# A two-layer pairwise block: the input projections of both layers rewritten as two row tiles

## The reference, cut to what matters

```python
x = x + conv(_ln_c(x), L0...)          # layer 0
t = t + scan(_ln_t(t))                 # recurrent, over 1024 steps
x = x + conv(_ln_c(x), L1...)          # layer 1
t = t + experts(_ln_t(t))

def conv(z, mask, ...):
    m  = mask[..., None]
    zn = _layer_norm(z, ln_in_w, ln_in_b)
    a  = m * sigmoid(zn @ w_ag + b_ag) * (zn @ w_ap + b_ap)
    b  = m * sigmoid(zn @ w_bg + b_bg) * (zn @ w_bp + b_bp)
    p  = einsum('bikc,bjkc->bijc', a, b)
    x  = _layer_norm(p, ln_out_w, ln_out_b) @ w_z + b_z
    g  = sigmoid(zn @ w_g + b_g)
    return x * g
```

## Time and profile before

| | us |
|---|---|
| median of 3 runs | 2461.65 (2459.01 to 2465.18) |
| profiled execution, whole / span | 2468.82 / 2467.1 |
| project, layer 0: first to last product | 44.7 to 365.8 |
| project, layer 1: first to last product | 1112.3 to 1509.2 |
| share of the span: PE, PEld, DVE, ACT, POOL | 80%, 53%, 67%, 41%, 56% |

### The profile page before, as it was taken

One profiled execution on the slowest core, in us unless ns is written; L12 is line 12 of the kernel. 1 busy time (PEld: TensorE's weight loads), 2 busy tenths in 40 slices (PEclk: granted clock), 3 DMA queues, 4 the chain that ended last, 5 costly groups with the idle time before them and its releaser, 6 DMA issues. The chain is left out here.

```text
span 2467.1 us, 47350 instructions
## 1 busy us (share of the span) xinstructions
PE 1973.2 (80%) x11760; PEld 1303.4 (53%) x11760; DVE 1640.9 (67%) x4305; ACT 1015.5 (41%) x2240; POOL 1380.7 (56%) x1657
## 2 busy tenths in 40 slices
PE   4999994888846668928989884888774899999998
PEld 2555553777732227815555552788763444444443
DVE  3777760555667778827777763166573788888887
ACT  1555551333314557903444432333323555444541
POOL 3999980566766760007777773177685434333330
PEclk9999996999988998959999997999976789998999
DMA  1565644888853321945777673698865555555552
GB/s 50 140 162 144 168 130 128 254 282 276 276 180 99 96 77 41 192 105 176 205 207 207 190 230 99 176 311 296 277 223 159 154 150 157 150 154 155 157 141 74
DMA packets 479516, 422.52 MB, mean 171 GB/s; under 512 B 229036, under 2 KB 376492, under 8 KB 479404
## 3 DMA queue, kind: packets, MB, share of 16 engines
q1 hardware_dynamic: 354476, 253.42, 37.8%
q10 hardware_dynamic: 124928, 167.81, 20.2%
HBM read 236.56 MB, written 150.99 MB: 157 GB/s over the span
## 5 line engine op out<-in xcount | busy, mean ns | idle before, releaser
L532 PE MATMUL cp_pv<-cp_weight,cp_zt 128*128 128x512 f32 x1024 | 536.0, 606 | 0.8 <-ACT cp_zt L563 0.8
L256 POOL TENSOR_TENSOR cc_ln_rstd<-cc_ln_var,numbers 128x8 f32<-128x8 f32 x128 | 255.5, 1996 | 196.8 <-DVE cc_ln_var L247 187.6
L256 POOL TENSOR_TENSOR cp_ln_rstd<-cp_ln_var,numbers 128x8 f32<-128x8 f32 x128 | 228.6, 1786 | 239.9 <-DVE cp_ln_var L247 238.6
L1467 DVE TENSOR_TENSOR ex_xe<-ex_spread,ex_xd 128x512 f32<-128x512 f32 x512 | 322.9, 683 | 40.5 <-PE ex_spread L1709 39.8
L719 PE MATMUL cc_sum<-a_res,cc_bch 128*128 (+1 forms) x2048 | 300.9, 296 | 58.4 <-DMA cc_bch<-b_scratch 56.3
L581 ACT ACTIVATE cp_sig<-cp_pv 128x256 f32<-128x256 f32 x512 | 193.7, 383 | 369.8 <-PE cp_pv L532 354.3
L533 PEld LDWEIGHTS cp_pg<-cp_weight,cp_zt 128*128 128x128 f32 x1024 | 198.3, 194 | 252.0 <-issue 252.0
L424 DVE TENSOR_TENSOR cp_prod<-cp_pv,cp_sig 128x256 f32<-128x256 f32 x512 | 207.2, 419 | 161.6 <-ACT cp_sig L581 133.9
L719 PEld LDWEIGHTS cc_sum<-a_res,cc_bch 128*128 128x128 f32 x2048 | 270.6, 205 | 82.4 <-issue 74.5
L809 ACT ACTIVATE cc_p<-cc_sum 128x512 f32 (+1 forms) x128 | 135.9, 1061 | 382.2 <-PE cc_sum L719 262.6
L1726 PE MATMUL ex_po<-ex_xe,ex_expert 128*64 128x512 f32 x1024 | 272.4, 656 | 0.1
(11 more groups left out here) (209 smaller groups left out, 3274.2 us busy)
## 6 DMA issues: line engine op xcount, KB each, us to landing
cc_bch<-b_scratch SPq DMA_DIRECT2D x256, 256.0 KB, 3.9
gate_scratch<-cp_gs ACTq DMA_DIRECT2D x128, 256.0 KB, 2.5
b_scratch<-cp_b_stage SPq DMA_DIRECT2D x256, 128.0 KB, 2.8
cc_g<-gate_scratch ACTq DMA_DIRECT2D x128, 256.0 KB, 4.5
after_conv<-cc_p ACTq DMA_DIRECT2D x128, 256.0 KB, 3.8
ex_xd<-ex_xt SPq DMA_DIRECT2D x256, 128.0 KB, 2.5
cp_x<-in_x SPq DMA_DIRECT2D x64, 256.0 KB, 3.3
cc_p<-in_x ACTq DMA_DIRECT2D x64, 256.0 KB, 3.6
```

Source lines behind the costliest of these rows:

```text
L256: pool.tensor_tensor(rstd[q][:], var[q][:], numbers[:, 0:1].to_broadcast([P, tiles]), ALU.pow).then_inc(scaled if shifts else known, 1)
L532: pe.matmul(pv[i][:], tokens, weight[:, 0:8 * C], start=True, stop=True).then_inc(v_made, 1)
L1467: dve.tensor_tensor(xe[u.mod(2)][:, :, h, i * P:(i + 1) * P], pb[2 * (p % 2) + h][:].rearrange("p (e t) -> p e t", e=EP), xd[u.mod(8)][:, ...
```

## The change

The project stage is rewritten; the rest is kept but for the layout of b in DRAM.

- **Weights.** The host packs the five matrices, gain, offset and biases of each layer into one array; `fold_weights` loads it with one DMA and folds it with one matmul. The weight is now the same 64 x 320 matrix on partitions 0 to 63 and 64 to 127.
- **Projections.** A row is two matmuls of 64 contraction rows and 320 columns, one for each half h, into two PSUM banks. Three such pairs of banks (`pv`) are taken in turn; `tp` and `ty` have a bank each.
- **One sigmoid.** ACT makes `ag`, `bg` and `g` of a row in one instruction of 384 numbers into `sig`, of which there are two (one per unit in turn). The gate is stored straight from `sig`, and on SP's queue; the sum of layer 1 is stored on SP's queue too.
- **Products and masks.** DVE writes the products of a row straight into `a_res` and `b_stage` (two instructions of 128 numbers), and POOL multiplies both by the mask in place (512 numbers once, 256 numbers twice for each unit).
- **The norm.** Statistics of four units are gathered. DVE makes a first guess of the reciprocal square root from the bits (three instructions of 32 numbers), POOL refines it by three Newton steps and makes a lift (14 instructions of 32 numbers for four units). ACT normalises the rows of half 0 and DVE those of half 1, four instructions of 64 numbers each per unit.
- **Order.** All engines run the same step s (`unit_steps`, loop body of 16 steps), each with its own offsets; x has eight buffers, y one.
- **b in DRAM** is laid out `[chunk, p, k, block, i, c]`; it is stored in four pieces of 256 KB per half and block, and a chunk is read in pieces of 1 KB.

```diff
-                    pe.matmul(pv[i][:], tokens, weight[:, 0:8 * C], start=True, stop=True).then_inc(v_made, 1)
-                    ins = pe.matmul(pg[q][:, i * 2 * C:(i + 1) * 2 * C], tokens, weight[:, 8 * C:],
-                                    start=True, stop=True)
...
+                    for h in range(H):
+                        half = slice(h * HALF, (h + 1) * HALF)
+                        pe.matmul(pv[slot(u, i)][:, h, 0:COLS], zt[u.mod(2)][half, i * P:(i + 1) * P], weight[half, :],
+                                  start=True, stop=True).then_inc(v_made, 1)
...
+                def gates(u, i):
...
+                    if i == 0 and (u - 2).real:
+                        act.wait_ge(gate_stored[u.mod(2)], u.div(2) * 16)
+                        act.wait_ge(prod_made, (u.n - 1) * R)
+                    act.wait_ge(v_made, (u.n * R + i + 1) * H)
+                    act.activation(sig[u.mod(2)][:, :, :, i, :].rearrange("p k h c -> p h k c"),
+                                   pv[slot(u, i)][:, :, 0:3 * C].rearrange("p h (k c) -> p h k c", k=3),
+                                   ACT.Sigmoid).then_inc(sig_made, 1)
...
+                def store_sum(u):
...
+                    sp.wait_ge(summed, u.n + 1)
+                    sp.dma_start(x[:, :, row_block(u), :], xs[u.mod(8)][:]).then_inc(sum_stored[u.mod(8)], 16)
+
+                def store_gate(u):
...
+                    sp.wait_ge(sig_made, u.n * R + R)
+                    sp.dma_start(gate_dram[:, :, row_block(u), :], sig[u.mod(2)][:, 2]).then_inc(gate_stored[u.mod(2)], 16)
...
+                def step(s):
+                    load(s + 9)
+                    store_sum(s + 8)
+                    store_gate(s - 1)
+                    store_b(s - 1)
```

The four other engines run these steps (VectorE, GpSimd, ScalarE, TensorE):

```diff
+                def step(s):
+                    product(s, 0)
+                    normalise(s + 2)
+                    product(s, 1)
+                    add_y(s + 8)
+                    measure(s + 8)
+                    product(s, 2)
+                    product(s, 3)
+                    if s.mod(4) == 3:
+                        first_guess(s + 5)
...
+                def step(s):
+                    mask_a(s - 1)
+                    if s.mod(4) == 0:
+                        refine(s + 4, 0)
+                    if s.mod(4) == 1:
+                        refine(s + 3, 1)
+                    mask_b(s - 1)
...
+                def step(s):
+                    gates(s, 0)
+                    gates(s, 1)
+                    normalise(s + 2, 0)
+                    gates(s, 2)
+                    take(s + 1)
+                    gates(s, 3)
+                    normalise(s + 2, 1)
...
+                def step(s):
+                    project(s, 0)
+                    turn_y(s + 8)
+                    project(s, 1)
+                    flip(s + 1)
+                    project(s, 2)
+                    project(s, 3)
```

More of the change, by code:

```diff
@@ L272, in quads, with __init__, __add__, __sub__ @@
         unit(G - 4 + j, G // 4 - 1, j, 3 - j)
-def quads_peeled(eng, unit):
-    for j in range(4):
-        unit(j, 0, j, 3, j > 0)
-    with eng.Fori(1, G // 4 - 1) as t:
-        for j in range(4):
-            unit(t * 4 + j, t, j, 3, True)
-    for j in range(4):
-        unit(G - 4 + j, G // 4 - 1, j, 3 - j, True)
-def conv_project(nc, tag, x, mask, w, a_res, b_dram, gate_dram, ident, numbers, parts=None):
-    W_COLS = 10 * C
+class Unit:
+    def __init__(self, turn, base, looped, body):
+        self.turn, self.base, self.looped, self.body = turn, base, looped, body
+    def __add__(self, k):
+        return Unit(self.turn, self.base + k, self.looped, self.body)
+    def __sub__(self, k):
+        return self + -k
+    def div(self, m, k=0):
+        return self.turn * (self.body // m) + (self.base + k) // m
+    def mod(self, m):
+        return self.base % m
+    @property
+    def n(self):
+        return self.turn * self.body + self.base
+    @property
+    def real(self):
+        return self.looped or 0 <= self.base < G
@@ new lines, in unit_steps, with fold_weights, _ @@
+def unit_steps(eng, step, first, last, head, tail, body=8):
+    for s in range(first, first + head):
+        step(Unit(0, s, False, body))
+    turns = (last + 1 - tail - first - head) // body
+    with eng.Fori(0, turns) as t:
+        for j in range(body):
+            step(Unit(t, first + head + j, True, body))
+    for s in range(first + head + body * turns, last + 1):
+        step(Unit(0, s, False, body))
+def fold_weights(nc, tag, packed, cols, weight, bank):
+    with Scope(nc, tag) as m:
+        pack = m.sb("pack", [P, P + 2 + cols])
+        fold = m.sb("fold", [P, P])
+        loaded, made, folded = m.sem("loaded"), m.sem("made"), m.sem("folded")
+        with nc.Block() as block:
+            @block.sync
+            def _(sp):
+                sp.dma_start(pack[:], packed).then_inc(loaded, 16)
+            @block.vector
+            def _(dve):
+                dve.wait_ge(loaded, 16)
+                dve.tensor_scalar(fold[:], pack[:, 0:P], pack[:, P:P + 1], pack[:, P + 1:P + 2], ALU.mult, ALU.add
+                                  ).then_inc(made, 1)
+                dve.wait_ge(folded, 1)
+                dve.tensor_scalar(weight, bank[:, 0:cols], 1.0 / C, None, ALU.mult).then_inc(made, 1)
+            @block.tensor
+            def _(pe):
+                pe.wait_ge(made, 1)
+                pe.matmul(bank[:, 0:cols], fold[:], pack[:, P + 2:], start=True, stop=True).then_inc(folded, 1)
@@ new lines, in step @@
+                def step(s):
[3 more added lines that the diff above has]
+                    store_b(s - 1)
+                run(sp, step)
+                for q in range(2):
+                    sp.wait_ge(b_stored[q], B_STORED * (NB // 2))
+                    sp.wait_ge(gate_stored[q], 16 * (G // 2))
+                if parts:
+                    for q in range(8):
+                        sp.wait_ge(sum_stored[q], 16 * (G // 8))
@@ L462, in _, with add_y @@
-                quads(dve, unit)
+                def add_y(u):
+                    if not parts or not u.real:
+                        return
+                    dve.wait_ge(x_in[u.mod(8)], u.div(8) * 16 + 16)
+                    dve.wait_ge(y_turned, u.n + 1)
+                    to = xs[u.mod(8)][:].rearrange("p h i c -> p i h c")
+                    dve.tensor_tensor(to, ty[:].rearrange("p (i h c) -> p i h c", i=R, h=H), to, ALU.add
+                                      ).then_inc(summed, 1)
@@ L538, in _ @@
-                if parts:
-                    pe.sem_inc(zt_made, 1)
-                turn_y(0, 0, 0)
-                turn_y(1, 0, 1)
-                flip(0, 0)
-                turn_y(2, 0, 2)
-                def unit(u, t, j, ahead):
-                    if ahead > 2:
-                        turn_y(u + 3, t + (j + 3) // 4, (j + 3) % 4)
-                    for i in range(R):
-                        if i == 2 and ahead:
-                            flip(u + 1, (j + 1) % 2)
-                        project(u, j % 2, i)
```

511 lines of the change are left out of this document (259 added, 252 removed).

## The result

The changed kernel takes 2471.3 us (median of 20 runs, 2457.52 to 2479.49), the kernel before 2462.9 (20 runs, 2453.37 to 2472.74): a ratio of 1.0034, 95% interval 1.0020 to 1.0047. It is slower by 8 us, where 29 were forecast. The sign was right and the size was not, and the stages show that the small number is a sum of large ones. The table takes the stages out of the two profiled executions, which lie 1 us apart and not 8 (2468.82 and 2469.76 us); "forecast" is the term of the prediction.

A forecast was written before the change was run, and what follows sets the result against it. VectorE was to pace layer 0 and a ring through the gate's store layer 1. Terms 12 + 38 - 17 - 8 - 4 + 8 = +29 us gave 2498 on the profiled execution, 2491 on the median; range 2390 to 2550.

The forecast's parts named there:

- What bounds the kernel, and what is relieved: Project stage: TensorE and GpSimd are full before; afterwards a row on two tiles takes 0.58 us and TensorE is no bound.
- Starts and ends: Before the first product: -17 us in layer 0, -8 in layer 1; ends of both layers' products: -4 together.
- Layer 0, the turns: Layer 0 products: VectorE and GpSimd wait out each other's instructions, normalising takes 2.1 us, a unit 5.2; +12 us.
- I take no change: TensorE's granted clock in the project stage: it stays as it was, as a stretch busy 64% ran at 1.00.
- The ring of 6.8: Layer 1 products: sigmoids wait for the gate's store, queued behind the sum's store and VectorE's add; 6.8 us a unit, +38.
- The combine stages: Both combine stages read b in 1 KB pieces: between 0 and 17 us more, the middle taken, +8.
- No turns: Rival: normalising is let through between GpSimd's instructions, layer 0 products 294 us, whole 2433 or 2439; chance 0.20.
- The ring doesn't bind: Rival, layer 1: stores land sooner, VectorE bounds it at 5.9 us a unit, 378 us, whole 2434; chance 0.14.
- The case of both: Rival: normalising is let through and layer 1 is not held by the gate's store; some 2390 us; chance 0.06.
- Strided writes: Rival: VectorE pays for strided products into `a_res`, 0.44 us a unit in layer 0 (+28), +14 in layer 1; 2533; chance 0.08.
- The gate's store lands late: Rival, layer 1: the store takes 3.5 us in place of 2.6, a unit 7.7, 58 us more; 2549; chance 0.05.
- Tiles that don't overlap: Rival: TensorE needs 5.0 and 5.6 us a unit, hidden, 2491 still; chance 0.05, together with a faster case.

The follow-up runs named there:

- e4: Changed kernel with VectorE's four normalising instructions moved from behind the unit's first product to behind its third; 2399.4 us, ratio 0.9723.
- e6: Changed kernel without GpSimd's masks (a's multiplication left out, b's cut to four numbers a unit), order and waits kept; 2429.8 us, ratio 0.9855.
- e2: Kernel before the change with only the new layout of b, so chunks are read in pieces of 1 KB; 2495.2 us, ratio 1.0105.

## Why the prediction was wrong in size

**What bounds the kernel, and what is relieved.** Right. TensorE and GpSimd were full and are not; the row on two tiles has a pitch of 0.54 us against 0.58 from the earlier trace rows.

**Starts and ends.** Right to a microsecond: -17.7 for -17, -7.3 for -8, -3.5 for -4 (the earlier trace rows against a first product at 27.0 in layer 0 and 39.0 us into layer 1).

**Layer 0, the turns.** The mechanism was right (e4, e6), the size was not. Up to the last look-ahead a unit takes 4.96 us for 5.2: the normalising is 1.63 us on average in place of 2.1, since the mask of a takes 1.04 and not 1.3, and the products of a row have a pitch of 0.41 for 0.45. VectorE was forecast to be full, and is busy 87% of the time. Part of the unit is a cost that the prediction ruled out: one unit in four takes 6.4 us on average, and behind ten of TensorE's fourteen pauses the clock is at half, 44 us in all. "I take no change" of the clock rested on the mean busy share of one stretch, 64% at full clock; here the share is higher (76%) and the clock still falls. With the late normalising it is 77%, one pause is over 1.5 us, and the clock stays at 1.00. The mean share was no ground for the forecast.

**The step that failed in both layers: a steady period times 64.** The last seven or eight units have nothing to load, add or measure, and nothing to normalise for later. Two of them in layer 0, one unit apart:

```profile
325.08 0.38 DVE L528 TENSOR_TENSOR a_res<-cp_pv,cp_sig 128x128 f32<-128x128 f32 x1 [0.84 <-ACT cp_sig L657]
...
329.10 0.39 DVE L528 TENSOR_TENSOR a_res<-cp_pv,cp_sig 128x128 f32<-128x128 f32 x1 [0.84 <-ACT cp_sig L657]
```

4.02 us. In layer 1 the ring is open there too, because no sum is left to be stored: 56 units at 6.72 us, 376 in all, and 30 us for the next seven. The ring of 6.8 was a good forecast for the unit (6.72) and a bad one for the stage: 435 against 408.8. Of the 26 us missing, some 18 are those last seven units, 5 the period, the rest the last unit, which ends with its last product. In layer 0 the 24 us are 14 of period, 8 of those units, and the last unit's end.

**The combine stages.** Forecast +8 with a range of 0 to +16; measured +31.5, and 29 for the layout alone (e2). The bound was put on the landing of a chunk, "a tenth of the landing at one chunk in six". The landing did rise by only 0.2 us of 3.9. But with three buffers for the chunks and TensorE waiting 28.5 us for them already in one stage (a wait that was in the trace and not among the rows looked at), there was no slack to hide it: that wait grew by 16.5 us in the first stage.

The three misses are -24, -26 and +24; the last hid half of the others. So the sign was right by luck: the two stages of products, forecast at +50, came to 0, and with the forecast +8 for the combine stages in place of +31.5 the changed kernel would have been some 15 us faster than the one before (8.4 - 23.5). The rest of the difference, +3.9 in the scan stage and -5.9 among the experts, is in code that did not change. The kernel before with the new layout has 588 us for the experts too, and the others 586 to 592, so the new projections are not the cause of the -5.9; what is stays open. The scan stage has 338 to 341 us in all kernels with the new projections and 337 in both with the old ones; that stays open too.

**The rivals.** No turns: not so in the changed kernel, and its layer 0 (294) was priced 20 us too high: without masks it has 274. The ring doesn't bind: wrong. The case of both was also added up wrong: by its own terms (-27 and -58 in place of +12 and +38) it is 2356, not 2390, so the range should have begun there. Strided writes: the product into `a_res` does take 0.37 us against 0.27 into `b_stage`, as priced, but the next begins 0.2 us after it all the same. The gate's store lands late: not so, the median is 2.6 us in layer 1, as it was before. Tiles that don't overlap: they do overlap. But "2491 still" was the worst-priced line of the prediction, as it took the clock to stay up: with one tile the kernel takes 3087, 616 us over the changed kernel, at half clock. The prediction priced a clock of 0.50 for two tiles only (6.4 us a unit).

## What to carry to other kernels

The period of a pipeline may be forecast to 2% (6.8 for 6.72), and the stage still be off by 6%: count the units at its end apart, in which the look-ahead is over, since half of the steps are missing from them. When a buffer is shared by a result and its store, follow the store's place in its queue: a store of something else, which waited for a step made late, held this one, and putting it first gave 55 us. A kernel that is far slower than its column count says may be at half clock: compare the duration of one instruction with the same one in a stretch of known clock. Of two engines that exclude each other, the cheap fix is the order within the unit: four small instructions moved behind the other engine's burst gave the same 35 us as taking the burst away.

## What the runs showed of the hardware

Two fp32 matmuls of 64 contraction rows and 320 columns on different row tiles take 0.54 us together at a granted clock of 1.00 and 1.07 at 0.50; on the same tile they take 2.13 at 0.50. Reading DRAM in pieces of 1 KB in place of 2 KB cost 17.0 and 20.5 us in stages of 347 of which the first was at 243 GB/s (e2), though the median landing of a chunk rose from 3.9 to 4.2 us only. TensorE's granted clock fell from 1.00 to 0.50 (1.2 GHz) soon after a pause of 1.7 us and was back at 1.00 at 205.5, some 4 us later, in a stage where the engine was busy 76% of the time; with the normalising moved it stayed at 1.00. With both matmuls on one row tile it was at 0.50 through 705 us in which TensorE was busy for 703.7. ScalarE's instructions in a row take less than the sum of their durations: the thirteen of a unit, 6.6 us in all in the kernel where it normalises both halves (means of 0.48, 0.53 and 0.63), had a period of 4.63.
